# Softmax key sums in two accumulators per unit: GpSimd adds key tiles in place, GpSimd's DMAs merge them, TensorE sums twice per unit

## What is computed

```python
scores = jnp.einsum('bhsd,bhtd->bhst', q, k) / math.sqrt(HEAD_DIM)
scores = scores + _band_mask(S, scores.dtype)      # 0.1 where |s - t| <= 2
attn = jax.nn.softmax(scores, axis=-1)
out = jnp.einsum('bhst,bhtd->bhsd', attn, v)
```

## Time and profile before

| | us |
|---|---|
| median of 3 runs | 4730.73 |
| lowest and highest | 4729.35, 4734.55 |
| the profiled execution | 4733.77 |
| its span, first to last instruction | 4731.9 |
| granted TensorE clock, mean | 0.987 |

### The profile page before, as it was taken

One profiled execution on the slowest core, in us unless ns is written; L12 is line 12 of the kernel. 1 busy time (PEld: TensorE's weight loads), 2 busy tenths in 40 slices (PEclk: granted clock), 3 DMA queues, 4 the chain that ended last, 5 costly groups with the idle time before them and its releaser, 6 DMA issues. The chain is left out here.

```text
span 4731.9 us, 68176 instructions
## 1 busy us (share of the span) xinstructions
PE 4630.4 (98%) x24976; PEld 2572.3 (54%) x24976; DVE 3346.7 (71%) x5663; ACT 2446.4 (52%) x4652; POOL 2820.4 (60%) x2207
## 2 busy tenths in 40 slices
PE   7999989999999999999999999999999999996999
PEld 6888844444444444444444444444444444434777
DVE  6444477777777777777777777777777777744776
ACT  2222226666666666666666666666666666661211
POOL 2111037777777777777777777777777777780000
PEclk9999979999999999999999999999999999998999
DMA  7655531112121212121212112111212121104443
GB/s 253 212 202 201 197 89 37 50 48 54 41 58 36 61 31 63 32 61 43 57 39 53 50 41 53 41 50 49 54 42 58 36 61 31 30 15 174 166 158 118
DMA packets 250862, 372.60 MB, mean 79 GB/s; under 512 B 36545, under 2 KB 103105, under 8 KB 245442
## 3 DMA queue, kind: packets, MB, share of 16 engines
q1 hardware_dynamic: 250562, 368.66, 26.2%
HBM read 211.82 MB, written 156.24 MB: 78 GB/s over the span
## 5 line engine op out<-in xcount | busy, mean ns | idle before, releaser
L699 DVE TENSOR_REDUCE part_max<-ps_m 128x1 f32<-128x512 f32 x4096 | 2547.8, 683 | 842.4 <-PE ps_m L595 840.6
L770 POOL TENSOR_TENSOR pair<-p_sb 128x512 f32<-128x512 f32 x2048 | 2565.9, 1283 | 920.6 <-ACT p_sb L687 597.0
L687 ACT ACTIVATE p_sb<-ps_s 128x512 f32<-128x512 f32 x4096 | 2114.8, 603 | 1288.4 <-PE ps_s L615 1225.2
L615 PE MATMUL ps_s<-q_st,k_st 97*128 97x512 f32 x4096 | 1728.5, 424 | 6.8 <-ACT p_sb L687 6.8
L595 PE MATMUL ps_m<-k_st,q_st 96*128 96x512 f32 x4096 | 1636.8, 403 | 21.6 <-POOL k_st L762 20.1
L615 PEld LDWEIGHTS ps_s<-q_st,k_st 97*128 97x128 f32 x4096 | 773.0, 189 | 1010.8 <-ACT p_sb L687 452.0
L629 PE MATMUL ps_o<-p_sb,v_sb 128*32 128x512 f32 x8192 | 1090.7, 605 | 0.0
L595 PEld LDWEIGHTS ps_m<-k_st,q_st 96*128 96x128 f32 x4096 | 786.2, 192 | 186.3 <-DVE part_max L699 29.2
L639 PE MATMUL ps_d<-pair,ones 128*32 128x512 f32 x4096 | 534.0, 593 | 3.8 <-POOL pair L770 3.8
L629 PEld LDWEIGHTS ps_o<-p_sb,v_sb 128*32 128x32 f32 x8192 | 161.3, 108 | 349.9 <-ACT p_sb L687 295.4
L166 POOL TENSOR_TENSOR xb<-xin,bo_row 128x2048 f32<-128x2048 f32 x16 | 75.5, 4716 | 428.1 <-DMA xin<-in_x 417.3
(11 more groups left out here) (93 smaller groups left out, 2631.9 us busy)
## 6 DMA issues: line engine op xcount, KB each, us to landing
q_st<-q_hi_d SPq DMA_DIRECT2D x128, 256.0 KB, 4.2
k_st<-k_hi_d SPq DMA_DIRECT2D x128, 256.0 KB, 4.9
xin<-in_x SPq DMA_DIRECT2D x16, 1024.0 KB, 8.4
xb_d<-xb SPq DMA_DIRECT2D x16, 1024.0 KB, 5.1
q_hi_d<-s_hi SPq DMA_DIRECT2D x64, 256.0 KB, 2.0
q_lo_d<-s_lo SPq DMA_DIRECT2D x64, 256.0 KB, 2.3
k_hi_d<-s_hi SPq DMA_DIRECT2D x64, 256.0 KB, 2.3
k_lo_d<-s_lo SPq DMA_DIRECT2D x64, 256.0 KB, 2.6
```

What stands on the lines that cost most here:

```text
L615: nc.tensor.matmul(ps_s[:, (HG * s + h) % RING_S, :], k_st[0:ROWS + 1, unit // QC % 2, kt // TT, h, kt % TT * P:(kt % TT + 1) * P], q_st[0 ...
L687: nc.scalar.activation(p_sb[:, s % SLOTS, h, :], ps_s[:, (HG * s + h) % RING_S, :], ACT.Exp, scale=SCALE).then_inc(p_ready, 1)
L699: nc.vector.tensor_reduce(part_max[:, unit % 2, col, n:n + 1], ps_m[:, seq % RING_M, :], AX.X, ALU.max).then_inc(max_taken, 1)
L770: nc.gpsimd.tensor_tensor(pair[:, m % PAIR_RING, h, :], p_sb[:, s % SLOTS, h, :], p_sb[:, (s + 1) % SLOTS, h, :], ALU.add).then_inc(paired, 1)
```

## The change

`pair` (four tiles of 4 heads by 512) becomes `acc`, two accumulators for each of two units, of the same size. Per unit, pairs 0 and 1 are added by GpSimd into accumulators 0 and 1. Pairs 2 to 7 are added in place, the odd tile onto the even tile in `p_sb`, and a DMA issued by GpSimd adds the result to accumulator n % 2 in SBUF. The add is now one instruction over all four heads. In place it needs the even tile to have been weighed, so that it waits for `pv_done`. ScalarE waits for the merge before it fills an even slot again. TensorE sums accumulator 0 at kt = 4 and accumulator 1 at kt = 6 of the unit after. The copies and DMAs of the sums move: ScalarE's `copy_sum` from kt = 4 to 7 and `o_high` from 14 to 13, SyncE's `store_sum`, `load_den` and `store_rec` from kt = 4, 6, 9 to 7, 8, 10; GpSimd's `scale_o` and `o_low` from behind pairs 5 and 6 to behind pairs 4 and 5.

```diff
-    PAIR_RING = 4
+    MERGES = PAIRS // 2 - 1
+    SUM_AT = (4, 6)
+    merged = [sem(f"merged{i}") for i in range(2)]
+    def merges_to(m):
+        return MERGES * (m // PAIRS) + m % PAIRS // 2
-        pair = sb("pair", [P, PAIR_RING, HG, CH])
+        acc = sb("acc", [P, 2, 2, HG, CH])
@@ sync
-                        if kt == 4:
+                        if kt == 7:
                             store_sum(unit - 1)
-                        if kt == 6:
+                        if kt == 8:
                             load_den(unit - 1)
-                        if kt == 9:
+                        if kt == 10:
                             store_rec(unit - 1)
@@ tensor
-            def add_keys(m):
-                unit, n = m // PAIRS, m % PAIRS
+            def add_keys(unit, n):
                 if n == 0:
                     at_least(pe, sum_copied, unit)
-                pe.wait_ge(paired, HG * (m + 1))
+                pe.wait_ge(merged[n], 16 * MERGES * (unit + 1))
                 for h in range(HG):
-                    last = nc.tensor.matmul(ps_d[h * HD:(h + 1) * HD, :], ones[:], pair[:, m % PAIR_RING, h, :],
-                                            start=(n == 0), stop=(n == PAIRS - 1))
+                    last = nc.tensor.matmul(ps_d[h * HD:(h + 1) * HD, :], ones[:], acc[:, unit % 2, n, h, :],
+                                            start=(n == 0), stop=(n == 1))
-                if s >= 4 and s % 2 == 1:
-                    add_keys(s // 2 - 2)
+                if s >= KT and s % KT in SUM_AT:
+                    add_keys(s // KT - 1, SUM_AT.index(s % KT))
@@ scalar
-                if kt == 4 and unit > 0:
+                if kt == 7 and unit > 0:
                     copy_sum(unit - 1)
-                if kt == 14 and unit > 0:
+                if kt == 13 and unit > 0:
                     o_high(unit - 1)
                 if s >= SLOTS:
+                    old = (s - SLOTS) // 2
                     act.wait_ge(pv_done, s - SLOTS + 1)
-                    act.wait_ge(paired, HG * ((s - SLOTS) // 2 + 1))
+                    act.wait_ge(paired, old + 1)
+                    if s % 2 == 0 and old % PAIRS > 1:
+                        act.wait_ge(merged[old % 2], 16 * merges_to(old))
@@ gpsimd
-                at_least(pool, sum_done, m - PAIR_RING + 1)
-                for h in range(HG):
-                    nc.gpsimd.tensor_tensor(pair[:, m % PAIR_RING, h, :], p_sb[:, s % SLOTS, h, :],
-                                            p_sb[:, (s + 1) % SLOTS, h, :], ALU.add).then_inc(paired, 1)
-                if m % PAIRS == 5 and m > PAIRS:
-                    scale_o(m // PAIRS - 1)
-                if m % PAIRS == 6 and m > PAIRS:
-                    o_low(m // PAIRS - 1)
+                unit, n = m // PAIRS, m % PAIRS
+                p_even, p_odd, total = p_sb[:, s % SLOTS], p_sb[:, (s + 1) % SLOTS], acc[:, unit % 2, n % 2]
+                if n < 2:
+                    at_least(pool, sum_done, 2 * (unit - 2) + n + 1)
+                    nc.gpsimd.tensor_tensor(total, p_even, p_odd, ALU.add).then_inc(paired, 1)
+                else:
+                    pool.wait_ge(pv_done, s + 1)
+                    nc.gpsimd.tensor_tensor(p_even, p_even, p_odd, ALU.add).then_inc(paired, 1)
+                    at_least(pool, merged[n % 2], 16 * (merges_to(m) - 1))
+                    pool.wait_ge(paired, m + 1)
+                    pool.dma_start(total, p_even, accum_op=ALU.add).then_inc(merged[n % 2], 16)
+                if n == 4 and unit > 0:
+                    scale_o(unit - 1)
+                if n == 5 and unit > 0:
+                    o_low(unit - 1)
```

More of the change, by code:

```diff
@@ L647, in _ @@
                 ahead(1, j)
-            for s in range(ST + 4):
+            for s in range(ST + SUM_AT[1] + 1):
                 if s < ST:
@@ L665, in copy_sum @@
             def copy_sum(unit):
-                act.wait_ge(sum_done, PAIRS * (unit + 1))
+                act.wait_ge(sum_done, 2 * (unit + 1))
                 at_least(act, o_out, 32 * unit)
```

## The result

| | before | after |
|---|---|---|
| median, 4 runs each (us) | 4730.83 (4729.35 to 4734.55) | 5088.65 (5080.41 to 5092.28) |
| ratio, 95% interval | 1 | 1.0753 [1.0734, 1.0771] |
| `attend`, us a unit, first to last score | 56.07 | 61.58 |
| granted TensorE clock, mean of the span | 0.987 | 0.933 |

The prediction said 4685 us, 4530 to 4850, and was wrong in the sign; the slowest rival that it named ended at 4885. 56.07 us a unit is taken from the first score of the first step to the first score of the last step (3585.9 us of the earlier trace rows run to the last step's fourth score, and give 56.09); 61.58 is the same after. The difference, 5.5 us x 64 = 353 us, is the whole of the 358 us: all of it lies in `attend`.

What follows compares the result with a forecast made beforehand. TensorE was taken as the bound at 56.1 us a unit; a floor of 51.0 plus 4.2 of losses gave 55.2, 58 us less over 64 units, plus 10 at the end: 4685 us, range 4530 to 4850.

Steps and rivals of the forecast that it cites:

- The key sums' price: On TensorE: one `add_keys` costs 0.85 us; removing six of eight per unit saves 5.1 us a unit.
- GpSimd's add and issue: On GpSimd: one add over 128x2048 takes 4.6 us, issuing a DMA 1.0 us; 46.6 us a unit with the rest.
- The rival of the slow issue: On GpSimd: an issue costs 2 us or more, 4775 us at 2.0 us; chance 0.15.
- The held bands: VectorE's bands wait for the whole GpSimd add; TensorE loses 1.8 us per held full pair, 0.7 per held edge.
- hardly held: Rival: a long GpSimd instruction lets VectorE's bands in between; 52.7 us a unit, 4526 us; chance 0.13.
- ScalarE's `o_high`: Before the exponentials of kt = 13, it waits for `scale_o`; TensorE loses 0.8 to 0.9 us.
- Merges, taken as hidden: DMAs of 1 MB within SBUF take 8 us each; pair 6, the tightest, has 8.9 us.
- merges land late: Rival: waits on `merged` before an even slot is filled delay the exponentials; 4755 to 4885 us; chance 0.22.
- The DMA share of 0.19: In `attend` before the change: taken as room for the merges, against the rival that they land late.

Runs made afterwards that it cites:

- e11: Kernel before, with one long add per pair and GpSimd itself adding one pair per unit into its neighbour, no DMA: 4675.24 us, ratio 0.9880.
- e12: Kernel before, with one long add per pair and GpSimd itself adding seven pairs in four units into their neighbours, no DMA: 4643.95 us, ratio 0.9814.
- e5: Changed kernel with each merge moving 256 KB (one head's tile) in place of 1 MB, bands kept: 4756.62 us.
- e7: Changed kernel with merges of 256 KB in place of 1 MB and VectorE's bands left out: 4490.49 us.
- e1: Changed kernel without the load of the reciprocals; `scale_o` adds the output to itself instead: 4818.72 us, ratio 1.0186.
- e6: Changed kernel with VectorE's bands left out, full merges of 1 MB kept: 5041.42 us.
- e10: Changed kernel with full merges, without the load of the reciprocals and without the bands: 4627.47 us, ratio 0.9779.
- e13: The same kernel as e10 once more (changed kernel, full merges, no load of the reciprocals, no bands), one run: 4617.95 us.
- e9: Kernel before, with one long add per pair and GpSimd itself adding two pairs per unit into their neighbours, no DMA: 4739.73 us, ratio 1.0019.
- e14: Changed kernel with merges of 256 KB, without the band of 8 elements at kt = 3 of units with u = 1: 4744.73 us.
- e2: Changed kernel without the load of the reciprocals, each GpSimd add of 128x2048 cut into four of 128x512: 4927.61 us, ratio 1.0414.
- e4: Changed kernel with two output tiles, three accumulators, output scaled and stored a unit later, sums copied at kt = 11: 5077.72 us, ratio 1.0744.

## Why the prediction was wrong

- **The key sums' price was right.** 0.85 us each: L645 136.6 us, and e11 and e12 gained it (56.5 and 88.7 us where 54 and 95 were due).
- **GpSimd's add and issue were right.** 4.6 us was 4594 ns; an issue, taken as 1.0, cost 0.88, and 0.55 us of waiting for the own add ahead of it. The rival of the slow issue is out: 875 ns against the 1.5 us at which it was to show.
- **The held bands were right in kind; the size agrees partly by luck.** Means went to 1150, 1111 and 1261 ns; "hardly held" is out. The prediction's terms for bands average 3.7 us a unit; e5 against e7 gives 4.3. But the clock, for which it had no term, is in the 4.3. e5 spends 244 us more than e7 at the lower level, and where the same wait came with and without the fall, 3.4 us at that level cost 1.6 (7.09 against 5.46). By that the clock makes some 115 us of the 266, an estimate, and the holding alone about 2.3 us a unit. By u (medians, e5 less e7) it is 5.6, 5.7, 4.7 and 1.8, where 2.4, 3.65, 4.3 and 4.3 were said. The rule of the Trainium skill that was cited (SBUF — State Buffer, Who interferes with whom) holds for adds of 4.6 us too; this trace agrees.
- **The step that failed: "ScalarE's `o_high`", 0.9 us.** It walked from the add over the issue to `scale_o` at T + 7.1, and took for granted that the reciprocals were there. That load is a DMA of its own which before landed 4.6 us after its issue and now meets six merges of 1 MB a unit. It landed after 9.8 us, and with the clock behind it the step kt = 13 grew to 9.25 us on the mean of the four u, 5.9 over its plain 3.32, where the prediction's sum has 0.5 (0.9, 0.9, nothing and 0.3). The rest of the walk was right: without the load, in e1, the same step grew by 0.84, 0.86, 0 and 0.02. e1 puts it at 270 us with the bands, and e6 against e10 at 414 without.
- **"Merges, taken as hidden" failed too**, at the place that was named as tightest. The margin of 8.9 us was right; the 8 us were a median (8.5 measured, 6.9 to 13.5), and pair 6 is not a median merge: it is issued behind the output's stores and the q loads. e10 against e7 gives 137 us, in e1 against e5 62. In the changed kernel as it is, the exponentials' waits for merges are 63.9 us against 161.5 in e13, probably since the stall at kt = 13 comes first. The rival "merges land late" was thus real, with 1.1 to 3.1 us a unit said and 2.0 found (e13: 54.25 against 52.23 us a unit), but it went only by the slots of p, and not by the other DMAs that the merges delay.
- **No term for the clock.** Every loss was counted as long as its wait. In e9 a wait of 2.46 us cost 7.1 us, in e5 one of 1.24 us cost 3.1 where the clock fell and 1.5 where it did not. It doesn't fall behind each wait: in e7 TensorE stands for 1.0 us at kt = 13 of nearly every unit, at a cost of 1.1, and the clock fell behind four of them. The kernel before never let TensorE wait between 1000 and 4000 us, so its trace could not show this.
- **The DMA share of 0.19 was read as room.** It is a mean of before. The merges add 402.68 MB of packets in 39.3% of the engines' time, and in the stretch that decides, the share was 0.92.

The parts are not a sum. From e7's 4490 us the bands alone add 266, full merges without the reciprocals' load 137, full merges with it 551, and everything 598. The late load covers the bands.

Still open: why the clock fell behind some held bands and not behind others of the same length (e5, e14), why a band is sometimes held over several GpSimd instructions (e2), whether fewer bytes or smaller packets helped in e5, and how the loss of e4 divides. Pairs written out of place, which would take the gate from the changed kernel, were not tried.

## What to carry to other kernels

When a change adds large DMAs, don't only ask whether they land in time for their own readers: list each small transfer that some engine waits for, and put the length of a large one ahead of it. A wait of TensorE of one to two and a half microseconds cost here little more than its own length where the clock held (e5, e7), and 2.5 to 3 times its length where the clock fell behind it (e5, e9), so a step that brings work on TensorE down by 0.85 us must not risk one. And moving an add from TensorE to GpSimd paid nearly in full (88.7 of 95 us, 1.9%) where GpSimd did it itself, away from the full bands and from `scale_o`, up to the first merge that made anything late.

## What was unexpected in the hardware

- A load of 256 KB issued by SyncE 1.1 us behind a merge of 1 MB did not move a packet for 5.2 us (1993.17 to 1998.35), until the merge was nearly through.
- A DMA that adds 1 MB within SBUF: 128 packets of 8 KB, about 0.65 us each, 6.9 / 8.5 / 13.5 us (min, median, max) from issue to landing.
- TensorE fell to its lower level behind idle times of 1.24 us (e5, nine units of sixteen) and 2.46 us (e9, all sixteen units with u = 1), and stayed there for 3.4 us and about 10 us though it was busy. Behind 1.8 us at kt = 10 of u = 2 it fell within the step in one unit of sixteen in the changed kernel and in eleven of sixteen in e5.
- A VectorE instruction of 8 elements with two SBUF inputs was held for 3.98 us, over four GpSimd adds that followed each other without a pause (e2).
- In one execution of e10 the granted clock was 0.65 and later 0.75, neither of the two levels, for most of the program, and the kernel took 5662.9 us instead of 4627.
